# Expert rows: a gather through a token table in place of 64 dispatch scatters

## What is computed

```python
x2 = rmsnorm(hid, ln2_w).reshape(-1, h)                  # 2048 x 256
probs = softmax(x2 @ gate_w.T)                           # 16 experts
top_w, top_i = top_k(probs, 4); top_w /= sum(top_w)
gu = einsum('th,eih->tei', x2, w1); g, u = gu[..., :176], gu[..., 176:]
down = einsum('tei,ehi->teh', silu(g) * u, w2)
routed = einsum('te,teh->th', wfull, down)               # wfull: top_w at top_i, else 0
sg, su = split(x2 @ sh_gu_w.T, 352)
shared = (silu(sg) * su) @ sh_down_w.T
return hid + routed + shared
```

## Time and profile before

| what | value |
|---|---|
| median of 3 runs (range) | 1999.33 us (1997.53 to 2004.32) |
| the profiled execution, its own time | 1989.11 us |
| its span, first to last instruction | 1987.3 us |
| mean granted TensorE clock | 0.922 of full speed |
| PE / DVE / ACT / POOL busy | 87% / 59% / 48% / 27% of the span |
| first block from the indices on | 1655 to 1756 us |
| second block | 1756 to 1987 us |

### The profile page before, as it was taken

The page is one execution under the profiler, slowest core; times in us unless marked ns, Lnnn a source line. Parts: engine busy times, 40 slices in busy tenths (PEclk is TensorE's granted clock), DMA queues, the critical chain, the costliest instruction groups (busy, mean ns, idle before and its releaser), DMA issues. The chain is left out here.

```text
span 1987.3 us, 34326 instructions
## 1 busy us (share of the span) xinstructions
PE 1722.4 (87%) x11668; PEld 1455.4 (73%) x11668; DVE 1165.0 (59%) x2625; ACT 951.5 (48%) x2452; POOL 529.5 (27%) x527
## 2 busy tenths in 40 slices
PE   7998897697699999999992999999999969259993
PEld 6666664555688888888881788888888867258883
DVE  4688884698655656566546555555555457335553
ACT  2577776486355444545541444444454423225442
POOL 4133321243311111111111111111121114736663
PEclk7699997898899999999996999999999968679997
DMA  4111121265100100100002101001000043447666
GB/s 142 55 34 29 29 70 40 78 252 213 43 13 1 43 12 13 43 1 11 1 1 77 43 1 32 12 12 29 5 12 1 1 117 108 147 101 139 126 115 162
DMA packets 73274, 117.40 MB, mean 59 GB/s; under 512 B 8285, under 2 KB 59021, under 8 KB 71943
## 3 DMA queue, kind: packets, MB, share of 16 engines
q1 hardware_dynamic: 54014, 89.03, 14.4%
q0 software_dynamic: 14448, 19.80, 5.6%
q10 hardware_dynamic: 4648, 6.38, 1.0%
HBM read 86.65 MB, written 44.70 MB: 66 GB/s over the span
## 5 line engine op out<-in xcount | busy, mean ns | idle before, releaser
L1812 ACT ACTIVATE da_prob<-da_prob,da_nb,d_rqs 128x128 f32<-128x128 f32 x256 | 123.3, 483 | 260.2 <-DVE da_nb L2072 260.2
L1812 ACT ACTIVATE hold_wq<-hold_wq,ca_nb,c_rqs 128x128 f32<-128x128 f32 x256 | 123.4, 483 | 235.4 <-DVE ca_nb L2072 235.4
L653 DVE TENSOR_REDUCE a_mx<-a_s 128x2 f32<-128x512 f32 x256 | 167.1, 681 | 60.5 <-PE a_s L541 58.7
L470 ACT ACTIVATE a_prob<-a_s 128x512 f32<-128x512 f32 x256 | 147.4, 600 | 85.7 <-PE a_s L554 85.4
L1874 POOL TENSOR_TENSOR hold_wq<-hold_wq,ca_rsum 128x512 f32<-128x512 f32 x64 | 66.7, 1042 | 428.3 <-DVE ca_rsum L2077 428.3
L1874 POOL TENSOR_TENSOR da_prob<-da_prob,da_rsum 128x512 f32<-128x512 f32 x64 | 66.6, 1041 | 422.9 <-DVE da_rsum L2077 422.9
L2700 POOL DMA_INDIRECT slot_results<-t_ysb,t_dest x79 | 124.3, 1574 | 91.7 <-ACT t_ysb L2714 42.8
L554 PE MATMUL a_s<-a_qs,a_ks 32*128 32x256 f32 x512 | 101.6, 346 | 32.4 <-ACT a_prob L470 32.3
L1884 PE MATMUL da_qk<-d_xTh,da_wqkv_h 128*128 128x512 f32 x256 | 106.7, 417 | 6.4 <-DVE da_wqkv_l L2023 6.4
L541 PE MATMUL a_s<-a_ks,a_qs 32*128 32x256 f32 x512 | 101.0, 351 | 3.1 <-DVE a_mx L653 3.0
L2084 DVE SCALAR_TENSOR_TENSOR ca_oT_l<-ca_oT,ca_bv,ca_oT_h 128x512 fp32r<-128x512 f32 x64 | 48.0, 751 | 93.3 <-ACT ca_oT_h L1826 93.3
(11 more groups left out here) (412 smaller groups left out, 5610.2 us busy)
## 6 DMA issues: line engine op xcount, KB each, us to landing
t_xg<-slot_rows SPq DMA_DIRECT2D x79, 144.0 KB, 2.5
mw_raw<-in_d_expert_w SPq DMA_DIRECT2D x16, 352.0 KB, 6.1
slot_results<-in_d_fill SPq DMA_DIRECT2D x1, 4608.0 KB
a_heads<-a_osb SPq DMA_DIRECT2D x128, 32.0 KB
a_wraw<-a_heads SPq DMA_DIRECT2D x32, 128.0 KB, 2.1
mw_down<-in_d_expert_d SPq DMA_DIRECT2D x1, 2816.0 KB
hold_wk<-in_c_wkT SPq DMA_DIRECT2D x1, 2064.0 KB
hold_wq<-in_c_wqT SPq DMA_DIRECT2D x1, 2064.0 KB, 9.0
```

The costliest lines, as they stand in the source:

```text
L470: act.activation(prob[:, w % PR, :, :], s2[w % 2][:, :, :], ACT.Exp, scale=1.0 / A_ROOT)\
L653: dve.tensor_reduce(mx[:, b % 2, :, h], s1[s1_use(b, u) % S1_BANKS][:, :, :], AX.X, ALU.max)\
L1812: ins = act.activation(prob[:, p, b, :], prob[:, p, b, :], ACT.Exp, bias=nb[:, p, b:b + 1], scale=rqs[:, r:r + 1], accum_out=sums[:, p, b: ...
```

## The change

Nothing is scattered in the first block. The normalised rows (272 numbers now: x and 16 weights, no token number) are stored once, as they stand, by one plain DMA into a DRAM tensor `token_rows` whose row 0 is blank. A token table is made on the chip: for each tile and each of its 128 places, the number of the token that belongs there. DVE writes for each batch two one-hot arrays in bfloat16 by equality (`locate`: place within a tile, 128 x 512, and tile, 128 x 320), ACT multiplies the second by the token's lane and by its batch (`name`: two of 128 x 320), and PE adds their products over 64 matmuls of 160 columns (`find`), in the shared expert's units 2 to 9. After unit 10's products DVE reads the table (`identify`): `ids` for the gather, `dest` for the later adding scatters. POOL then gathers 128 rows by `ids` for each tile: 16 tiles in the first block, 8 ahead of the loop of the second, and the other 55 within that loop, each behind the adding scatter of tile t, for tile t+24. SP's 79 loads are gone. In the second block DVE's three small operations for each tile become one. Of the 24 buffers for rows 16 take the place of `rows` and 8 lie in `raw`. `hid` now shares its memory with `silu`. The filling of `slot_rows` shrinks from 80 x 128 rows to one.

The diff, cut to its core:

```diff
@@ bit_linear_ffn, SP
-                sp.dma_start(slots.rearrange("(u r) n -> u r n", r=Y_BUFS * P),
-                             fill.unsqueeze(0).broadcast_to([TABLE // Y_BUFS, Y_BUFS * P, ROW])).then_inc(filled, 16)
+                sp.dma_start(slots[0:1, :], fill[0:1, :]).then_inc(filled, 16)
@@ constants
-META = 2 * EXPERTS
-ROW = DIM + META
+ROW = DIM + EXPERTS
+X_EARLY = BATCHES
+X_BUFS = BATCHES + 8
@@ ExpertWeights
+    def gather(self, pool, slots, t):
+        pool.indirect_dma_start(self.tile(t), None, slots[:, :],
+                                bass.IndirectOffsetOnAxis(self.ids[:, t:t + 1], 0)).then_inc(self.x_in[t % X_BUFS], 16)
@@ sort_and_share, SP
+                sp.wait_ge(meta_ready, 1)
+                sp.wait_ge(xn_ready, BATCHES)
+                sp.dma_start(slots[1:1 + BATCHES * TOKENS, :].rearrange("(b p) c -> p b c", p=P), rows[:, :, :])\
+                    .then_inc(rows_stored, 16)
                 for n in range(RAW_BUFS, EXPERTS):
                     sp.wait_ge(first.w_lo, n - RAW_BUFS + 1)
                     first.load(sp, n)
@@ sort_and_share, POOL
-                for b in range(BATCHES):
-                    for k in range(TOPK):
-                        n = TOPK * b + k
-                        after(pool, sent_rows[n % IN_FLIGHT], 16 * (n // IN_FLIGHT))
-                        pool.indirect_dma_start(slots[:, :], bass.IndirectOffsetOnAxis(idx[:, b, k:k + 1], 0),
-                                                rows[:, b, :], None).then_inc(sent_rows[n % IN_FLIGHT], 16)
-                for k in range(IN_FLIGHT):
-                    pool.wait_ge(sent_rows[k], 16 * len(range(k, BATCHES * TOPK, IN_FLIGHT)))
+                pool.wait_ge(rows_stored, 16)
+                pool.wait_ge(turned_psum, PAIRS)
+                pool.wait_ge(ids_ready, 1)
+                for n in range(X_EARLY):
+                    if n >= IN_FLIGHT:
+                        pool.wait_ge(first.x_in[n - IN_FLIGHT], 16)
+                    first.gather(pool, slots, n)
@@ sort_and_share, PE
+                def find(b):
+                    pe.wait_ge(lane_ready, b + 1)
+                    pe.wait_ge(named_ready, 2 * b + 2)
+                    for k in range(TOPK):
+                        mm = pe.matmul(f_ps, in_lane[:, b % DEEP, k, :], named[:, b % DEEP, k, :, :].rearrange("p v c -> p (v c)"),
+                                       start=(b == 0 and k == 0), stop=(b == BATCHES - 1 and k == TOPK - 1),
+                                       skip_group_check=True)
+                    mm.then_inc(found_psum, 1)
...
+                    if 2 <= t < 2 + PAIRS:
+                        find(2 * (t - 2))
+                        find(2 * (t - 2) + 1)
@@ sort_and_share, ACT
-                    after(act, hid_ready, t - 1)
+                    after(act, hid_lo, t - 1)
...
+                def name(b):
+                    act.wait_ge(tile_ready, b + 1)
+                    act.wait_ge(ld_c, 32)
+                    after(act, found_psum, b - DEEP + 1)
+                    act.activation(named[:, b % DEEP, :, 0, :], in_tile[:, b % DEEP, :, :], ACT.Copy, scale=cons[:, P:P + 1])\
+                        .then_inc(named_ready, 1)
+                    act.activation(named[:, b % DEEP, :, 1, :], in_tile[:, b % DEEP, :, :], ACT.Copy, scale=float(b))\
+                        .then_inc(named_ready, 1)
...
+                    if 1 <= t < 1 + PAIRS:
+                        name(2 * (t - 1))
+                        name(2 * (t - 1) + 1)
@@ sort_and_share, DVE
-                dve.tensor_scalar(idx[:, :, :], first4[:, :, 0:TOPK], -1.0, None, ALU.add).then_inc(idx_ready, 1)
+                chained(dve.tensor_scalar(tile_of[:, :, :], first4[:, :, 0:TOPK], 1.0 / P, -64.5 / P, ALU.mult, ALU.add))
+                chained(dve.tensor_scalar(tile_of[:, :, :], tile_of[:, :, :], ROUND, None, ALU.add))
+                chained(dve.tensor_scalar(tile_of[:, :, :], tile_of[:, :, :], ROUND, None, ALU.subtract))
+                chained(dve.scalar_tensor_tensor(lane_of[:, :, :], tile_of[:, :, :], -float(P), first4[:, :, 0:TOPK],
+                                                 ALU.mult, ALU.add))
+                def locate(b):
+                    after(dve, found_psum, b - DEEP + 1)
+                    dve.tensor_tensor(in_lane[:, b % DEEP, :, :], lane_of[:, b, :].unsqueeze(2).broadcast_to([P, TOPK, P]),
+                                      lanes.unsqueeze(1).broadcast_to([P, TOPK, P]), ALU.is_equal).then_inc(lane_ready, 1)
+                    after(dve, named_ready, 2 * (b - DEEP + 1))
+                    dve.tensor_tensor(in_tile[:, b % DEEP, :, :], tile_of[:, b, :].unsqueeze(2).broadcast_to([P, TOPK, TABLE]),
+                                      times.unsqueeze(1).broadcast_to([P, TOPK, TABLE]), ALU.is_equal).then_inc(tile_ready, 1)
+                def identify():
+                    dve.wait_ge(found_psum, BATCHES)
+                    chained(dve.tensor_copy(found[:, :, :].rearrange("p v c -> p (v c)"), f_ps))
+                    chained(dve.scalar_tensor_tensor(wanted[:, 0, :], found[:, 1, :], float(P), found[:, 0, :],
+                                                     ALU.mult, ALU.add))
+                    dve.tensor_scalar(first.ids[:, :], wanted[:, 0, :], 1.0, None, ALU.mult).then_inc(ids_ready, 1)
...
+                    if t < PAIRS:
+                        locate(2 * t)
+                        locate(2 * t + 1)
...
+                    if t == PAIRS + 2:
+                        identify()
@@ routed_experts, SP (79 loads of rows out, the four loads of x0 stay)
-                    sp.dma_start(xg[:, t % X_BUFS, :], slots[P * t:P * t + P, :]).then_inc(x_in[t % X_BUFS], 16)
@@ routed_experts, POOL
+                for t in range(X_EARLY, X_BUFS):
+                    if t >= X_EARLY + IN_FLIGHT:
+                        pool.wait_ge(x_in[t - IN_FLIGHT], 16)
+                    first.gather(pool, slots, t)
                 for t in range(NT):
                     pool.wait_ge(y_copied, t + 1)
-                    pool.wait_ge(dest_ready, t + 1)
                     if t >= PLANES:
                         pool.wait_ge(sent[(t - PLANES) % Y_BUFS], 16 * ((t - PLANES) // Y_BUFS + 1))
...
+                    pool.indirect_dma_start(results[:, :], bass.IndirectOffsetOnAxis(first.dest[:, t:t + 1], 0),
+                                            ysb[:, t % Y_BUFS, :], None, compute_op=ALU.add).then_inc(sent[t % Y_BUFS], 16)
+                    if t + X_BUFS < NT:
+                        pool.wait_ge(xT_psum, t + 1)
+                        pool.wait_ge(picked, t + 1)
+                        first.gather(pool, slots, t + X_BUFS)
@@ routed_experts, DVE
-                    dve.tensor_tensor(both[:, :, :], xg[:, t % X_BUFS, DIM:ROW].rearrange("p (a e) -> p a e", a=2),
-                                      first.pick[:, t, :].unsqueeze(1).broadcast_to([P, 2, EXPERTS]), ALU.mult)\
-                       .then_inc(masked, 1)
...
+                    dve.tensor_tensor_reduce(weighed[:, t % 2, :], xg(t)[:, DIM:ROW], first.pick[:, t, :], 1.0, 0.0,
+                                             ALU.mult, ALU.add, wd[:, t % D_BUFS:t % D_BUFS + 1]).then_inc(picked, 1)
```

More of the change, by code:

```diff
@@ L2198, in __init__ @@
         self.pick = s.sb("pick", [P, TABLE, EXPERTS], BF16)
+        self.rows = s.sb("rows", [P, X_EARLY, ROW])
+        self.ids = s.sb("ids", [P, TABLE], mybir.dt.int32)
+        self.dest = s.sb("dest", [P, TABLE], mybir.dt.int32)
+        self.x_in = [s.sem(f"x_in{k}") for k in range(X_BUFS)]
         self.ld_d = s.sem("ld_d")
@@ L2221, in sort_and_share @@
     PAD = EXPERTS + 4
+    LANE = 1
+    DEEP = 4
     PAIRS = BATCHES // 2
@@ L2250, in sort_and_share @@
         rstd = s.sb("rstd", [P, BATCHES])
-        rows = s.sb("rows", [P, BATCHES, ROW])
+        rows = first.rows
         gw = s.sb("gw", [P, KT, 2, EXPERTS], F32R)
-        logits = s.sb("logits", [P, BATCHES, EXPERTS])
+        logits = wb[:, :].rearrange("p (b e) -> p b e", b=BATCHES)
         mx = s.sb("mx", [P, BATCHES])
@@ L2274, in sort_and_share @@
         silu = s.sb("silu", [P, 2, GT])
-        hid = s.sb("hid", [P, 2, GT])
+        hid = silu
         turned = [s.ps(f"turned{k}", [P, KT, 2, P]) for k in range(4)]
@@ L2294, in sort_and_share @@
         table_own = s.sem("table_own")
-        sent_rows = [s.sem(f"sent_rows{k}") for k in range(IN_FLIGHT)]
         def width(j):
@@ L2598, in _ @@
                 chained(ins)
-                dve.tensor_scalar(idx[:, :, :], first4[:, :, 0:TOPK], -1.0, None, ALU.add).then_inc(idx_ready, 1)
+                chained(dve.tensor_scalar(tile_of[:, :, :], first4[:, :, 0:TOPK], 1.0 / P, -64.5 / P, ALU.mult, ALU.add))
[16 more added lines that the diff above has]
+                    dve.tensor_scalar(first.ids[:, :], wanted[:, 0, :], 1.0, None, ALU.mult).then_inc(ids_ready, 1)
+                    chained(dve.tensor_tensor(wanted[:, 1, :], wanted[:, 0, :], offset, ALU.add))
```

(37 more changed lines are left out.)

89 lines of the change are left out of this document (43 added, 46 removed).

## The result

| | before | after |
|---|---|---|
| median of all runs on one chip | 1997.82 us (17 runs, 1985.67 to 2009.19) | 2008.3 us (17 runs, 2000.21 to 2017.18) |
| ratio to before | 1 | 1.0054, 95% interval 1.0032 to 1.0076 |
| span of the profiled execution | 1987.3 us | 2008.9 us |
| HBM written | 44.70 MB | 25.69 MB |

The changed kernel is slower by 0.54%, 10.5 us. Forecast were 2001.5 us and a range of 1984 to 2026.

The account below looks back on a forecast made before the run. The dispatch scatters on POOL hold up the second block, then PE leads at 2.27 us per tile. -24.2 + 32.7 - 6.5 = +2.0 us on 1989.1, with the median 10.2 us above that execution: 2001.5 us, range 1984 to 2026.

Parts of the forecast that it names:

- The price of a gather: On POOL, each gather of 128 rows was taken at 0.96 us like a plain scatter, 1.26 us with the gap.
- rival B: Slower: a gather costs up to the adding scatter's 1.55 us, giving 2043 us; decides from 1.02 us; chance 0.26.
- Rival C: Faster: a gather costs 0.32 us like SP's load, the loop stays at 139.5 us, giving 1970 us; chance 0.16.
- Stretch one: First block and start of the second, up to scatter 0: 1744.5 against 1768.75, -24.2 us.
- rival D: Slower: DVE leads the shared expert's units if equality into bfloat16 costs twice; +8 us makes 2010; chance 0.10.
- the term for the indices: First block: one 0.19 us operation becomes four chained ones of the like, +0.7 us.
- change of block: Between first and second block: the same 6.4 us as before, then PE starts at once, not 2.16 us later.
- Stretch two: Second block's loop, scatters 0 to 55: POOL leads at 3.13 us a tile, 172.2 against 139.5 us, +32.7 us.
- Stretch three: Second block, scatters 55 to 78, no gathers: POOL catches up for some five tiles, 54.5 us shrink to 48, -6.5 us.
- A: The forecast itself: POOL leads the loop and spends there what the first block saves; range 1990 to 2013; chance 0.48.

Follow-up runs that it names:

- e7: Kernel before with the token table built but used for destinations only; all 64 dispatch scatters and SP's 79 loads stay: 1996.25 us, ratio 1.0017.
- e1: Changed kernel without the 55 gathers in the second block's loop, so tiles 24 to 78 work on stale rows: 1966.58 us, 0.9815 of before.
- e4: Changed kernel with the loop's 55 gathers issued in groups of four behind every fourth scatter: 2020.03 us, ratio 1.0099 to before.
- e3: Changed kernel with DVE reading the token table one unit earlier, behind unit 9 instead of unit 10: 2000.63 us, ratio 1.000 to before.
- e2: Changed kernel with each of the loop's 55 gathers issued a second time, into a buffer nobody reads: 2080.86 us, ratio 1.040 to before.
- e5: Changed kernel with the result scatters writing instead of adding, so the sum over a token's experts is lost: 1967.8 us, 0.9882 of before.

## Why the prediction was right, and where its terms were off

| step | predicted | measured | |
|---|---|---|---|
| anchor to scatter 0 | -24.2 | -25.0 | two errors of opposite sign |
| 0 to 55 | +32.7 | +37.9 | gather and scatter longer when they alternate; first tile |
| 55 to 78 | -6.5 | -2.1 | hardly any catching up, and a slip in the sum |
| 78 to end | 0 | +1.2 | not explained: e7, which ends as before does, has 25.4, e1 to e4 have 25.4 to 25.6 |
| sum | +2.0 | +12.0 | medians: +10.5 |

**The price of a gather** was the deciding step, and it was right: 0.94 us behind its like and 0.99 in the loop, against 0.96 taken, both below the 1.02 from which rival B was to decide. Rival C is out with it. The plain scatter was the right row to lean on the earlier trace rows.

**Stretch one** agrees by luck in part. PE's eight `find` matmuls of a unit took 0.60 to 0.73 us (0.56 taken) and DVE's pair 1.1 us (1.0 taken), as costed, and so rival D didn't come. Yet the shared expert's last accumulation ended 8.0 us later behind the anchor, not 5.3, and the indices came at 50.2 us, where the prediction had 48.3. In the steady units the forecast holds: a unit takes 4.8 us, as said. So does the term for the indices: PE's first product behind the anchor starts at 3.0 us instead of 2.2 (0.7 taken). What was left out lies between them, some 2.4 us: PE pauses for ACT's and DVE's results (0.31 us at 1669.72, 0.26 at 1670.68), and the granted clock is 0.50 from 1668 to 1674, a low stretch of some 7 us, where before it lasted under 4 (0.62 and 0.53 from 1656 to 1660, 1.00 from there). The prediction had a term for neither. The 16 gathers took 23.6 us, 25.2 forecast. POOL was last by 5 us, exactly as said (1738.6 against DVE's 1733.6). The **change of block** then took 3.5 us (1738.63 to PE's 1742.16) instead of 6.4; e3 has 3.2. Why it is shorter isn't shown. SP's load can't be the reason, for the 6.4 ended where SP issued it; one difference is that POOL waited for the last scatters to land at the block's end, and doesn't wait for its gathers now.

The two lengthened gathers, 1.62 and 1.30 us at 1721.57 and 1723.50, lie within the 4.09 us in which DVE works through five low parts, each with two inputs in SBUF; the gathers around them took 0.95. The Trainium skill, SBUF — State Buffer, section Who interferes with whom, infers that a tensor_tensor doesn't stall descriptor generation. These rows speak against that inference here too, by 1.0 us on two gathers, and e3 has the same: 1.30 and 1.30 us at 1710.38 and 1711.98, within DVE's five low parts from 1708.37 on. With the earlier trace rows that is three executions in which the two coincide in time; no run takes DVE's work away from beside the gathers, so the cause isn't shown.

**Stretch two** held the step that failed, by size and not by mechanism: "1.55 + 0.30, and one gather, 0.96 + 0.30: 3.11 us a tile". Measured are 1.59 and 0.99, 3.20 us a tile over 54 tiles with the longer ones: +4.0 us. I had taken durations from rows in which each instruction follows its like. The other 1.2 us are the first tile, 4.34 us from scatter 0 to scatter 1. That POOL leads is shown from three sides: e2 doubles the gathers (+70 in this stretch, 69 by POOL's own time), e5 shortens the scatter (-34, 33 by POOL's own time), and e1 takes the gathers away (-41, down to the pace of the loop before). One sign was worded wrongly: "POOL over 90% busy up to scatter 55" came out at 80%, because the gaps don't count as busy; and PE, held to be 73% busy, was at 84%, at the lower clock.

The Trainium skill, DMA: Bandwidth & Descriptors, section SWDGE vs HWDGE vs iDMA, would have plain transfers issued by SP or ACT. e7 against after agrees: SP issues such a load in 0.32 us, and with these loads the loop is 138.4 us instead of 177.4, though at the price of the 64 scatters that make them plain.

**Stretch three** failed in "POOL catches up at 1.85 to 1.95 us a tile". It did so for one scatter (1930.73 to 1932.62). The chain in order of time shows why not longer:

```profile
1930.73 4.47 DMA slot_results<-t_ysb,mw_dest
...
1935.94 3.70 DMA slot_results<-t_ysb,mw_dest
```

Scatter 57 has to wait for the landing of scatter 55, which took 4.47 us, and scatter 59 for that of 57, 3.70 us. In the loop the gathers had covered this wait; without them two scatters take a landing and some 0.7 us, 4.4 to 5.2 us in all, or 2.2 to 2.6 a tile. That is PE's own pace of 2.28 us, and not the 1.85 to 1.95 that I took. My price of a scatter left out the wait that the prediction itself had named a few lines above. The lead of ACT's copies over the scatters was 8.9 us for tile 55 (1921.78 to 1930.73), 5.1 us for tile 59 (1935.29 to 1940.37) and 3.5 us for tile 78 (1979.69 to 1983.15). It shrank, but not into time won: the copies went on at 3.2 us a tile up to tile 62, most of them waiting for the landing of the scatter four tiles back. And the sum had a slip of its own: five tiles at 1.9 us and 18 at PE's 2.27 make 50.4 us, 4.1 less than before, and not the 48 that were put down; 2.4 of the 4.4 us missed here are that.

The forecast of the likeliest case stood at +2.0 us with the bound of 0.3% at 6; the terms that were off sum to 10.0 us (-0.8, +5.2, +4.4, +1.2), and carried it over that bound. "Slower" did have the largest chance, 0.42, but 0.36 of it stood on rivals B and D, which didn't come; this way, POOL leading with a gather at its forecast price, had 0.06. That the largest chance fell on the right side is luck. The median of 2008.3 us does lie within the range that A was given by itself, 1990 to 2013 (its own bounds, +6.4 for the gather, +5.5 for PE and +6.5 for the third stretch, add up to 2020 at the upper end).

## What to carry to other kernels

A queue that takes over work must be summed over the stretch it gets it in: taking the 64 scatters out of one stretch won 25 us, and the 55 gathers cost 38 in a loop where that engine had been 62% busy and each of its instructions drags a gap of 0.30 us. Before moving issue work onto an engine, add duration and gap of all that it issues for one tile and hold it against the leading engine's time for a tile; here 3.2 against 2.5 us. Take durations from rows in which the neighbour on the queue is the one that it will have.
